# A preparing stage dissolved into the steps of the first attention pass

## The reference, cut to what matters

```python
xn = layernorm(ctx, ln_x_g, ln_x_b)                 # 4096 x 256
ln = layernorm(_layernorm(x), ln_l_g, ln_l_b)       # 256 x 256, normalised twice
q  = ln @ Wq                                        # 16 heads of 64
kv = concatenate([xn @ Wkv, ln @ Wkv])              # 4352 keys
qn, kn = rmsnorm(q, qn_g) * 64 ** -0.5, rmsnorm(k, kn_g)
attn = softmax(qn @ kn.T  (masked))
x = x + (attn @ v) @ Wout + bout
x = x + performer_attention(_layernorm(x))          # untouched
x = x + experts(_layernorm(x))                      # untouched
```

## Time and profile before

| | us |
|---|---|
| median of three runs | 731.86 (731.55 to 732.55) |
| the profiled execution, its own time | 734.44 |
| its span, first to last instruction | 732.7 |
| busy in the span: TensorE | 655.9 (90%) |
| VectorE | 509.0 (69%) |
| ScalarE | 424.0 (58%) |
| GpSimd | 254.8 (35%) |

### The profile page before, as it was taken

The page is one execution under the profiler, slowest core; times in us unless marked ns, Lnnn a source line. Parts: engine busy times, 40 slices in busy tenths (PEclk is TensorE's granted clock), DMA queues, the critical chain, the costliest instruction groups (busy, mean ns, idle before and its releaser), DMA issues. The chain is left out here.

```text
span 732.7 us, 15695 instructions
## 1 busy us (share of the span) xinstructions
PE 655.9 (90%) x5846; PEld 564.3 (77%) x5846; DVE 509.0 (69%) x996; ACT 424.0 (58%) x977; POOL 254.8 (35%) x194
## 2 busy tenths in 40 slices
PE   1535999999999999999999999999995784999997
PEld 1425888888888888888888888888873672999997
DVE  5995677777686677767767768776775624676764
ACT  3445676766667666676666766667663301655741
POOL 2541433433243333334324333333320023246450
PEclk9956999999999999999999999999996755899999
DMA  6122600000000000000000000000003004165510
GB/s 205 58 58 62 194 2 2 2 22 1 2 22 2 1 2 22 2 1 24 1 2 22 3 1 5 6 1 2 2 2 115 1 0 144 54 208 172 173 55 15
DMA packets 27560, 30.59 MB, mean 42 GB/s; under 512 B 4313, under 2 KB 24930, under 8 KB 27490
## 3 DMA queue, kind: packets, MB, share of 16 engines
q1 hardware_dynamic: 24834, 28.26, 12.4%
q10 hardware_dynamic: 2656, 1.39, 0.6%
HBM read 29.38 MB, written 0.26 MB: 40 GB/s over the span
## 5 line engine op out<-in xcount | busy, mean ns | idle before, releaser
L839 POOL TENSOR_TENSOR k_rms<-k_ss,neg_half 128x4 f32<-128x4 f32 x136 | 164.4, 1221 | 299.1 <-DVE k_ss L781 298.7
L775 DVE SCALAR_TENSOR_TENSOR probs_sum<-probs,tile_mask,probs_sum 128x512 f32<-128x512 f32 x264 | 197.9, 750 | 98.5 <-ACT probs L727 94.6
L727 ACT ACTIVATE probs<-s_ps,minus_bound 128x512 f32<-128x512 f32 x272 | 164.9, 688 | 124.2 <-PE s_ps L645 124.2
L528 PE MATMUL kv_ps<-w_pair,xn 128*128 128x256 f32 x1632 | 212.6, 286 | 6.3 <-PEq L179 5.0
L528 PEld LDWEIGHTS kv_ps<-w_pair,xn 128*128 128x128 f32 x1632 | 198.6, 189 | 15.1 <-issue 5.2
L657 PE MATMUL o_ps<-probs,v 128*64 128x256 f32 x1088 | 132.6, 386 | 0.8 <-ACT probs L727 0.8
L645 PEld LDWEIGHTS s_ps<-q_parts,kt 64*128 64x128 f32 x1632 | 97.7, 184 | 27.9 <-issue 25.4
L645 PE MATMUL s_ps<-q_parts,kt 64*128 64x256 f32 x1632 | 111.1, 282 | 1.9 <-DVE kt L785 1.9
L657 PEld LDWEIGHTS o_ps<-probs,v 128*64 128x64 f32 x1088 | 71.7, 136 | 42.3 <-issue 11.2
L711 ACT ACTIVATE v<-kv_ps,tile_mask 128x128 f32<-128x128 f32 x272 | 87.8, 391 | 0.0
L703 ACT ACTIVATE k_sq<-kv_ps 128x256 f32<-128x256 f32 x136 | 53.4, 393 | 35.7 <-PE kv_ps L528 35.6
(11 more groups left out here) (182 smaller groups left out, 651.7 us busy)
## 6 DMA issues: line engine op xcount, KB each, us to landing
w_raw<-in_ffn_W SPq DMA_DIRECT2D x18, 1024.0 KB, 5.2
p_rows<-in_ctx SPq DMA_DIRECT2D x8, 512.0 KB, 3.8
w_raw<-in_L_xattn_Wkv SPq DMA_DIRECT2D x14, 128.0 KB, 2.4
p_wq_raw<-in_L_xattn_Wq ACTq DMA_DIRECT2D x1, 1024.0 KB, 6.3
wout<-in_L_xattn_Wout SPq DMA_DIRECT2D x8, 128.0 KB, 2.1
x_res<-in_x SPq DMA_DIRECT2D x1, 256.0 KB, 4.7
w_raw<-in_L_xattn_Wkv ACTq DMA_DIRECT2D x2, 128.0 KB, 3.2
f_Wq<-in_L_attn_Wq SPq DMA_DIRECT2D x1, 256.0 KB, 3.9
```

Source lines behind the costliest of these rows:

```text
L528: last = nc.tensor.matmul(out, stationary(k, s), moving(k, m), start=n == 0, stop=n == len(terms) - 1)
L727: nc.scalar.activation(probs[n % P_RING][:, :, c, :], s_ps[n % 2][c][:], ACT.Exp, bias=minus_bound[:]).then_inc(exp_done, 1)
L775: nc.vector.scalar_tensor_tensor(total, probs[n % P_RING][:, i], seen, total, ALU.mult, ALU.add).then_inc(sum_done, 1)
L839: nc.gpsimd.tensor_tensor(k_rms[n % 2][:].rearrange("p i c -> p (i c)"), k_ss[n % 2][:].rearrange("p i c -> p (i c)"), neg_half[:, 0:4], A ...
```

## The change

`prepare` is gone. Its work stands in `attention`, with these parts.

The key tiles are made in units of two, as the passes take them. Before the loop come units 0 to 4 or 6, according to the step; in pair m (now counted from 0, with e = 2m) the rest follows: `statistics` of e+7 and e+8, `center` of e+7 and e+8, transposes, `gain` and `rest` of e+5 and e+6. So pairs 0 to 4 have all of it, pair 5 only the last three steps. Normalising moves from VectorE (`tensor_scalar`) to ScalarE (`center`, Identity with scale `rstd` and bias `mean_off`, which VectorE computes in the new `offset`). The two layer norms of the latents become one root with other constants. The transposes go into `o_ps[1]`, which pass 0 does not use.

Queries are made for two passes (4 heads) at a time, in `o_ps[0]`: t = 0 before the loop, t = 1, 2, 3 in the middle of passes 1, 3 and 5, at pairs 13, 30 and 47 and the two pairs after each; the weights are split three pairs ahead. `q_parts` is a ring of two.

Queues: SyncE issues x and three groups of rows, `bout`, five more groups each after a wait on `z_done`, and then what it issued before; ahead of each second `load_weights` stands a load of query weights. ScalarE still issues 14 DMAs first, with `Wq` (now 256 KB) and the first `Wkv` ahead of the gains.

```diff
-            prepare(nc, sem, a, x_res, ...)
-            attention(nc, sem, a, x_res, ..., w_raw, w_pair, q_parts, tile_mask, minus_bound, xn, fw, ew)
+        attention(nc, sem, a, x_res, ident, ones, neg_half, fw, ew)
...
+        def source(u):
+            return x_res[:] if u == 0 else rows[(u + 1) // 2 % 3][:, (u + 1) % 2 * 2:(u + 1) % 2 * 2 + 2, :]
+        def query_pair(t, stage):
+            return ((2 * t - 1) * NU - 1) // 2 + 5 + stage
...
# TensorE
+            def transpose_z(u):
+                pe.wait_ge(z_done, u + 1)
+                if u:
+                    pe.wait_ge(affine_done, u)
+                for k in range(KD):
+                    for i in range(2):
+                        last = nc.tensor.transpose(zt_ps(k)[:, i * P:(i + 1) * P], z[u % 2][:, i, k * P:(k + 1) * P], ident[:])
...
+            transpose_z(0); transpose_z(1); project_q(0); transpose_z(2)
+            project(0); transpose_z(3); project(1); transpose_q(0); transpose_z(4)
+            for m in range(STEPS // 2 + 1):
+                e = 2 * m
+                if e + 5 < NU:
+                    transpose_z(e + 5)
                 for n in (e + 2, e + 3): project(n)
                 for n in (e, e + 1): transpose_k(n)
+                for t in range(1, NPASS // 2):
+                    if m == query_pair(t, 0):
+                        project_q(t)
+                    if m == query_pair(t, 1):
+                        transpose_q(t)
+                if e + 6 < NU:
+                    transpose_z(e + 6)
                 for n in (e - 2, e - 1): weight_v(n)
                 for n in (e, e + 1): scores(n)
...
# ScalarE
+            def center(u):
+                act.wait_ge(off_done, u + 1)
...
+                for i in range(2):
+                    last = nc.scalar.activation(z[u % 2][:, i, :], source(u)[:, i, :], ACT.Identity,
+                                                scale=rstd[u % 2][:, i:i + 1], bias=mean_off[u % 2][:, i:i + 1])
...
+            def gain(u):
+                act.wait_ge(zt_done, u + 1)
...
+                for k in range(KD):
+                    last = nc.scalar.activation(affine[u % 2][:, k].rearrange("p i n -> p (i n)"), zt_ps(k), ACT.Identity,
+                                                scale=gains[:, which, 0, k:k + 1], bias=gains[:, which, 1, k:k + 1])
+                last.then_inc(affine_done, 1)
+                act.wait_ge(affine_done, u + 1)
+                nc.scalar.activation(xn[:, 2 * u:2 * u + 2, :, 0, :].rearrange("p i k n -> p k i n"), affine[u % 2][:], ACT.Copy).then_inc(xn_hi, 1)
...
# ScalarE, the loop: weights(e-2), weights(e-1)
+                if e + 5 < NU:
+                    gain(e + 5)
                 square(e + 2); keep_v(e + 2); square(e + 3); keep_kt(e); keep_kt(e + 1)
+                if e + 6 < NU:
+                    gain(e + 6)
                 keep_v(e + 3)
+                for u in (e + 7, e + 8):
+                    if u < NU:
+                        center(u)
...
# VectorE
+            def offset(u):
+                dve.wait_ge(root_done, u + 1)
...
+                nc.vector.scalar_tensor_tensor(mean_off[b][:], mean_var[b][:, :, 0], -1.0, rstd[b][:], ALU.mult, ALU.mult).then_inc(off_done, 1)
+            def rest(u):
+                dve.wait_ge(xn_hi, u + 1)
...
+            for m in range(STEPS // 2 + 1):
+                statistics(e + 7)
                 add_weights(e - 2, 0); add_weights(e - 2, 1)
+                offset(e + 7); rest(e + 5)
                 mean_square(e + 2); add_weights(e - 1, 0); mean_square(e + 3)
                 kt_rest(e); kt_rest(e + 1)
+                statistics(e + 8)
                 add_weights(e - 1, 1); scale_k(e + 2); scale_k(e + 3)
+                offset(e + 8); rest(e + 6)
...
# GpSimd
+            for m in range(STEPS // 2):
+                root_of(e + 7); root(e + 2); root_of(e + 8); root(e + 3)
```

More of the change, by code:

```diff
@@ L626, in project, with project_q, transpose_q @@
                 last.then_inc(kv_done, 1)
+            def transpose_z(u):
[5 more added lines that the diff above has]
+                        last = nc.tensor.transpose(zt_ps(k)[:, i * P:(i + 1) * P], z[u % 2][:, i, k * P:(k + 1) * P], ident[:])
+                last.then_inc(zt_done, 1)
+            def project_q(t):
+                if t == 0:
+                    pe.wait_ge(xn_lo, 1)
+                else:
+                    pe.wait_ge(y_added, 2 * t - 1)
+                pe.wait_ge(wq_lo, t + 1)
+                for j in range(QT):
+                    last = part_products(nc, q_ps(j), lambda k, s: xn[:, j, k, s, :], lambda k, s: wq[:, k, s, :])
+                last.then_inc(q_done, 1)
+            def transpose_q(t):
+                pe.wait_ge(qn_done, t + 1)
+                for i in range(2):
+                    for j in range(QT):
+                        last = nc.tensor.transpose(q_ps(i)[:, j * P:(j + 1) * P], qn[:, j, i, :], ident[:])
+                last.then_inc(qt_done, 1)
             def transpose_k(n):
@@ L674, in project_out @@
                 last.then_inc(y_done, 1)
-            for m in range(-1, STEPS // 2 + 1):
-                a = 2 * m
-                for n in (a + 2, a + 3):
+            pe.wait_ge(ident_done, 1)
+            transpose_z(0)
+            transpose_z(1)
+            project_q(0)
+            transpose_z(2)
+            project(0)
+            transpose_z(3)
+            project(1)
+            transpose_q(0)
+            transpose_z(4)
+            for m in range(STEPS // 2 + 1):
+                e = 2 * m
+                if e + 5 < NU:
+                    transpose_z(e + 5)
+                for n in (e + 2, e + 3):
                     if exists(n):
@@ L698, in _ @@
         def _(act):
+            act.dma_start(wq_raw[:], wq_view(a)[0]).then_inc(wq_in, 16)
+            for s in range(2):
+                act.dma_start(w_raw[0][:, :, s * P:(s + 1) * P], wkv_view(a)[0, s]).then_inc(w_in[0], 16)
+            with nc.allow_non_contiguous_dma(reason="a vector onto partitions"):
+                for n, name in enumerate(("ln_l_g", "ln_l_b", "ln_x_g", "ln_x_b")):
+                    act.dma_start(gains[:, n // 2, n % 2, :], a["L0_xattn_" + name].rearrange("(k p) -> p k", p=P)).then_inc(gains_in, 16)
+                for n, name in enumerate(("qn_g", "kn_g")):
+                    act.dma_start(gq[:, n, :], a["L0_xattn_" + name].partition_broadcast(P)).then_inc(gq_in, 16)
+                    for c in range(2):
+                        act.dma_start(gq_col[c * DH:(c + 1) * DH, n:n + 1], a["L0_xattn_" + name].rearrange("(p o) -> p o", o=1)).then_inc(gq_in, 16)
@@ L699, in square, with keep_qt @@
+            def keep_qt(t):
+                act.wait_ge(qt_done, t + 1)
+                nc.scalar.activation(q_parts[t % 2][:, :, 0, :], o_ps[0][:], ACT.Copy, scale=gqk_col[:]).then_inc(qt_hi, 1)
             def square(n):
@@ L729, in weights_hi @@
             def weights_hi(g):
-                act.wait_ge(w_in[g % 2], 32 * ((g + 1) // 2))
+                act.wait_ge(w_in[g % 2], 32 * (g // 2 + 1))
                 nc.scalar.activation(w_pair[g % 2][:, :, 0, :], w_raw[g % 2][:], ACT.Copy).then_inc(w_hi, 1)
-            for m in range(-1, STEPS // 2 + 1):
-                a = 2 * m
-                for n in (a - 2, a - 1):
+            act.wait_ge(gains_in, 64)
+            center(0)
+            weights_hi(0)
+            center(1)
+            gain(0)
@@ new lines, in _ @@
+            queries_hi(0)
+            gain(1)
+            center(2)
+            gain(2)
+            square_q(0)
+            center(3)
+            square(0)
+            act.wait_ge(mask_done, 1)
+            keep_v(0)
+            gain(3)
+            square(1)
+            keep_v(1)
+            act.wait_ge(col_done, 1)
+            keep_qt(0)
+            center(4)
+            gain(4)
+            center(5)
+            center(6)
+            act.wait_ge(bound_done, 1)
+            for m in range(STEPS // 2 + 1):
+                e = 2 * m
+                for n in (e - 2, e - 1):
@@ L749, in _ @@
+                for t in range(1, NPASS // 2):
+                    if m == query_pair(t, 0):
+                        square_q(t)
+                    if m == query_pair(t, 1):
+                        keep_qt(t)
+                for n in (e, e + 1):
                     if 0 <= n // NU < NPASS - 1 and n % NU == 6:
@@ L753, in _, with link, statistics @@
         def _(dve):
+            count = [0]
+            def link(ins):
+                count[0] += 1
+                ins.then_inc(own, 1)
+                dve.wait_ge(own, count[0])
+            def statistics(u):
+                b = u % 2
+                if u == 0:
+                    dve.wait_ge(x_in, 16)
+                else:
+                    g = (u + 1) // 2
+                    dve.wait_ge(rows_in[g % 3], 16 * ((g - 1) // 3 + 1))
+                for i in range(2):
+                    last = nc.vector.bn_stats(stats[b][:, i, :], source(u)[:, i, :])
```

(74 more changed lines are left out.)

518 lines of the change are left out of this document (170 added, 348 removed).

## The result

| | before | after |
|---|---|---|
| median, us | 732.72 (6 runs, 731.55 to 734.58) | 729.20 (6 runs, 727.74 to 730.30) |
| span of the profiled execution | 732.7 | 728.4 |
| first scores at | 78.13 | 42.98 |
| scores of pair 5 at | 112.72 | 101.69 |
| last scores at | 548.33 | 544.61 |

The ratio is 0.9947, with a 95% interval of 0.9931 to 0.9964: 3.5 us faster in the medians, 4.3 in the spans of the two profiled executions. The spans divide into: first scores 35.15 earlier; pairs 0 to 5 58.71 us instead of 34.59, 24.1 more; from there to the last scores 442.92 instead of 435.61, 7.3 more; behind them 0.6 less. Together -4.3.

The account below looks back on a forecast made before the run. TensorE, full from the first scores on, was taken to bound the kernel, after a preparing stage led by VectorE. -33.6 + 23.0 + 6.3 = -4.3 us gave 727.5 us from 731.86, range 717 to 742.

Parts of the forecast that it names:

- The ring: Pairs 0 to 5: chain of waits through VectorE, GpSimd and ScalarE back to the second kt_rest, 11.4 us a pair.
- Head start: Prologue: first scores at 44.5 us instead of 78.13, a gain of 33.6 us, ends 29 to 36.
- The path: Prologue: longest in-order chain from ScalarE's first center at 13.0 us to the first scores, taken at 44.5.
- the two clocks that the forecast held open: Projects (2) and (3) in the prologue: first scores at 45.2 us with TensorE at 1.2 GHz, 43.3 at 2.4.
- its bounds: One center on ScalarE: between 0.62 and 1.0 us, taken as 1.0.
- Pairs 0 to 5: Start of pass 0: five intervals of 11.4 us instead of 6.9, plus a weight split, cost 23.0 us.
- the rule: GpSimd contends with VectorE's two-input instructions: roots in pairs 0 to 5 0.95 and 1.4 us, 2.3 us more in all.
- Queries: Passes 1, 3 and 5: 2.1 us of TensorE work each, 6.3 us in all, other engines' share hidden.
- Steady pairs changed: Sign that the forecast is wrong; pairs outside the start and the query work were to stay at 6.90 us.
- rival 1: Pairs 0 to 5: ScalarE's own 9.8 us binds; 23.0 becomes 15.0, time 719.5 us, chance 0.17.
- Rival 3: Pass 0: TensorE with gaps falls to 1.2 GHz and stays there, 16.0 us a pair, time 750, chance 0.15.
- the forecast's clock of 1.00: Sign in pass 0: TensorE's granted clock stays at 1.00.

Follow-up runs that it names:

- a1: Changed kernel with one unused tile of 32 bytes per partition ahead of rows: 724.69 us, ratio 0.9885 to the kernel before.
- a2: Kernel before the change with the same unused 32 bytes per partition ahead of w_raw: 732.74 us, ratio 1.0002.
- a3: Changed kernel with root(e+3) ahead of root_of(e+8) in GpSimd's list: 723.62 us, ratio 0.9876 to the kernel before.
- a4: Changed kernel with center(e+8) moved behind the next pair's exponentials on ScalarE: 720.84 us, ratio 0.9830 to the kernel before.
- b3: Changed kernel with each transpose of k done four times in pairs 1 to 5: 728.54 us, ratio 0.9924 to the kernel before.
- b2: Changed kernel without the query work and weight loads of t = 1, 2, 3: 724.17 us, ratio 0.9873 to the kernel before.
- b4: Changed kernel with root(e+3) first, late center(e+8), wait for gains moved to gain(0), and 32 unused bytes: 713.92 us, ratio 0.9740 to before.
- c1: b4 with its unused tile at 96 bytes instead of 32: 722.4 us, ratio 0.9858 to the kernel before.
- c2: b4 with 32 more unused bytes ahead of kt: 718.1 us in one run.
- c3: b4 with w_raw, w_pair and q_parts ahead of xn, at their addresses before the change: 721.3 us, ratio 0.9834 to the kernel before.

## Why the prediction was right

The ring bound pairs 0 to 5 as forecast, the query work cost TensorE's time alone, and the other work was hidden. The sizes were off in four places, and they offset each other.

**Head start**: 33.6 forecast, 35.15 measured. The first center came at 12.04 instead of 13.0: ScalarE's issues ended at 9.2 us, not 11.6, and the gains' DMA, not the queue, was the last wait. The next row shows it:

```profile
12.04 1.09 ACT L470 ACTIVATE z<-x_res,mean_off,rstd 128x256 f32<-128x256 f32 x2 [1.47 <-DMA gains<-in_L_xattn_ln_x_b]
```

The path then ran as written (sum of q's squares done 24.9, forecast 25.6; center(4) done 32.1, forecast 33.1), with a root of 8 columns at 2.09, not 1.8, and projects of pair 0 in 4.48 us, between the two clocks that the forecast held open. A center took 1.09, just above the upper end of its bounds. The 35.15 hold for one pair of executions: first scores came up to 1.6 us earlier in others (a1 41.37 for after's 42.98, and a2 76.98 for before's 78.13).

**Pairs 0 to 5**: 23.0 forecast, 24.1 measured. The ring was right as a mechanism (a3, a4) and in size (11.15 to 11.6 without the clock and 12.09 with the weight split, forecast 11.4 and 11.95). Within it the forecast had root_of(e+8) too short by 0.38 (0.75, measured 1.13) and root(e+3) too long by 0.15 (1.15, measured 1.00). On the small root the Trainium skill ("GPSIMD Engine Reference", Specifications: shared SBUF interfaces) had the better direction: the two-column root took 0.70 in pair 0, where no two-input addition runs beside it, and 1.13 in pairs 1 to 4, where one does; the interval grew by the same 0.4 (11.14 to 11.56). The other root met VectorE waiting, and took 1.00 and not the 1.4 that the forecast gave it by the rule. ScalarE's wait in front of center(e+8) was up to 1.9 us, not about 1.3. Of the 1.1 us, 0.75 is the clock, whose last fall was paid for, and 0.4 the sizes of the ring's terms (b3, without a fall, is 23.4 above before).

**Queries**: 6.3 forecast, 5.6 measured, with all of the rest hidden as forecast (b2). The product cost 1.42 instead of 1.56 and the transposes 0.45 instead of 0.53.

**Not in the forecast**: the 0.03 us of every steady pair, 1.7 us, where the forecast left every other pair at 6.90; and 0.6 less behind the last scores, where the code is untouched and the thirteen traces lie between 182.5 and 184.8 us. "Steady pairs changed" had been named as what would make it wrong; it did happen, small, and offset the better head start. That the sum came out to the tenth is chance: +1.55, -1.1, +0.7, -1.7 and +0.6 add up to nothing, and the first and the last change by as much from one execution to the next. The medians give 3.5, not 4.3.

**Rivals**: rival 1 (719.5) was not the change, but a4 (720.8) makes nearly that of it. Rival 3's mechanism showed in two of five intervals, against the forecast's clock of 1.00 in all of pass 0, but TensorE did not stay slow: weight_v took 3.33 and 3.56 us instead of 1.95, the scores behind it 1.68 at the full clock, and it cost 0.75 us of the 23. What the forecast held against it, that a slow TensorE has no gaps, fits: from 73.97 to 78.04 us TensorE ran without one.

## What to carry to other kernels

When a stage is dissolved into a loop, own work per engine is only the floor of an iteration: write down the ring of waits that returns to the same instruction, through every engine in whose order something stands behind something else, and sum it. Here a lightly used engine's order of two instructions was worth more than the whole change (5.6 us against 3.5). And ask of each delay whether it lies on the ring: the scores that the slow clock made late by 0.8 us were back in step one pair later, since the ring does not pass through them.

## What was not expected of the hardware

In four kernels that differ in nothing but the addresses of tiles in SBUF (b4, c1, c2, c3), 24 projecting matmuls took 2.83 to 2.97 us and 24 of scores 1.61 to 1.63 us; the kernel before has 2.93 and 1.56. The four ran in 713.9, 722.4, 718.1 and 721.3 us. That is 1.2%, more than twice the change that was to be judged.

The clock fell to 1.2 GHz in pass 0 without a long pause of TensorE: before the falls in the third and fifth interval no single wait was above 1.7 us. In a3, with waits for gain(e+5) of up to 1.6 us in intervals about 1.3 us shorter, it stayed at 2.4 GHz throughout; in which intervals it falls differs between kernels with the same ring (see above). Two intervals of a3:

```profile
41.50:51.50 10.00, 8.07 (x76) 6.59 (x76) 7.55 (x24) 9.90 (x24) 3.85 (x5) 1.00 0.17 52
51.50:61.80 10.30, 8.11 (x78) 6.64 (x78) 8.45 (x25) 9.62 (x23) 4.28 (x5) 1.00 0.50 151
```
